# A Mamba block with two MLPs on one core: chunks of 27 and 37 batches, three buffers for B, and one norm's squares ahead of decays

## What is computed

```python
h = _L0_tok_ref(x, L0_tok_W, L0_tok_b)                    # patches @ W.T + b, 512 features
h = h + _L0_attn_ref(_layernorm(h, axis=-1), ...)
h = h + _L0_ffn_ref(_layernorm(h, axis=-1), ...)          # silu(x@gate)*(x@up) @ down, hidden 2048

# inside _L0_attn_ref
zxbcdt = x @ in_proj_w.T
dt = jax.nn.softplus(dt_in @ dt_proj_w.T + dt_proj_b)
dA = jnp.exp(dt[..., None] * A)
def step(h, inp):
    dA_i, dBx_i, C_i = inp
    h = dA_i * h + dBx_i
    y = jnp.einsum('bgn,bgcn->bgc', C_i, h.reshape(b, GC, D_INNER // GC, D_STATE))
y = ys.transpose(1, 0, 2) + D_skip * x_full
h = res + (y * jax.nn.silu(z)) @ out_proj_w.T
return h + mlp(rmsnorm(h))                                # hidden 2048 again
```

## Time and profile before

| | |
|---|---|
| median of 3 runs | 679.44 us (677.98 to 681.44) |
| profiled execution | 676.66 us, of it the span from the first to the last instruction 674.7 us |
| mean granted clock of TensorE | 0.979 of 2.4 GHz |
| busy in the span | PE 630.5, PEld 505.2, DVE 425.5, ACT 329.3, POOL 428.9 us |
| chain that ended last | PE 73%, DVE 12%, ACT 4%, POOL 4%, issue 3%, DMA 2% |
| DMA | 163.50 MB, 242 GB/s over the span |
| loads of B, median from issue to landing | 32 of 580 KB 8.2 us, 32 of 700 KB 6.7 us |
| on the chain at the start | a load of B, 6.61 us from 31.14 |
| on the chain from 212.31 to 235.82 us | GpSimd, its products, additions and softplus one after another |

### The profile page before, as it was taken

The page is one execution under the profiler, slowest core; times in us unless marked ns, Lnnn a source line. Parts: engine busy times, 40 slices in busy tenths (PEclk is TensorE's granted clock), DMA queues, the critical chain, the costliest instruction groups (busy, mean ns, idle before and its releaser), DMA issues.

```text
span 674.7 us, 8618 instructions
## 1 busy us (share of the span) xinstructions
PE 630.5 (93%) x2846; PEld 505.2 (75%) x2846; DVE 425.5 (63%) x660; ACT 329.3 (49%) x646; POOL 428.9 (64%) x244
## 2 busy tenths in 40 slices
PE   4959998799999979999979999999999999999998
PEld 3637675466665657777747777766999998999998
DVE  4087997889987859889887988861322223332132
ACT  4358888458887363323346323321642443543441
POOL 0276786348787999887877988644455464445561
PEclk9979999799999979999989999999999999999999
DMA  8799997599999949989866998634443353144421
GB/s 339 253 358 365 316 312 245 169 280 371 336 375 373 362 176 359 412 334 332 316 247 231 345 326 317 200 124 113 140 153 127 124 157 125 63 128 131 147 67 43
DMA packets 49164, 163.50 MB, mean 242 GB/s; under 512 B 4320, under 2 KB 18528, under 8 KB 48480
## 3 DMA queue, kind: packets, MB, share of 16 engines
q1 hardware_dynamic: 49120, 162.95, 69.6%
HBM read 145.24 MB, written 17.69 MB: 242 GB/s over the span
## 4 chain that ended last, share of the span: by engine, by line
PE 73%; DVE 12%; ACT 4%; POOL 4%; issue 3%; DMA 2%; SPq 0%; DVEq 0%; ACTq 0%; POOLq 0%
PE work L990 53%; PE da L990 15%; DVE da L781 7%; PE work L1000 5%; DVE hs L792 3%; POOL hs L453 2%; ACT L528 1%; DMA bb<-b_rows 1%; ACT da L551 1%; DMA c_rows<-c_rows 1%; DMA sm<-small 1%; POOL acc L479 0%; POOL acc L477 0%; POOL hs L466 0%; DVE a L847 0%
## 5 line engine op out<-in xcount | busy, mean ns | idle before, releaser
L781 DVE TENSOR_TENSOR_SCAN da<-da,hs 128x290 f32<-128x290 f32 (+1 forms) x256 | 198.1, 817 | 35.1 <-POOL hs L453 21.2
L453 POOL TENSOR_TENSOR hs<-dtx,bb 128x1160 f32<-128x1160 f32 (+1 forms) x64 | 171.1, 2674 | 59.6 <-PE work L1000 52.4
L551 ACT ACTIVATE da<-dt,a_neg 128x261 f32<-128x261 f32 (+1 forms) x256 | 118.4, 495 | 144.7 <-DVE hs L792 144.5
L432 POOL TENSOR_TENSOR ws<-wraw,ws 128x1024 fp32r<-128x1024 f32 x40 | 101.5, 2538 | 92.8 <-ACT ws L559 92.8
L990 PE MATMUL work<-sq,wraw 128*128 128x290 f32 x512 | 126.0, 407 | 1.5 <-DVE sq L880 1.1
L990 PE MATMUL work<-hn,win 128*128 128x290 f32 (+1 forms) x336 | 103.6, 457 | 17.4 <-DVE hn L855 8.0
L990 PEld LDWEIGHTS work<-sq,wraw 128*128 128x128 f32 x512 | 96.5, 189 | 30.8 <-issue 1.8
L792 DVE TENSOR_TENSOR hs<-da,cb 128x580 f32<-128x580 f32 (+1 forms) x128 | 105.3, 822 | 10.2 <-DMA cb<-c_rows 3.5
L990 PEld LDWEIGHTS work<-hn,win 128*128 128x128 f32 x336 | 65.7, 200 | 51.3 <-issue 26.1
L559 ACT CAST ws<-wraw 128x1024 fp32r<-128x1024 f32 x48 | 50.3, 1048 | 70.6 <-PE da L990 34.4
L990 PE MATMUL work<-hn,ws 128*128 128x350 f32 x480 | 79.2, 323 | 1.6 <-DVE hn L951 1.6
(11 more groups left out here) (97 smaller groups left out, 630.8 us busy)
## 6 DMA issues: line engine op xcount, KB each, us to landing
wraw<-w_stream SPq DMA_DIRECT2D x104, 512.0 KB, 3.8
bb<-b_rows SPq DMA_DIRECT2D x32, 700.0 KB, 6.7
cb<-c_rows SPq DMA_DIRECT2D x32, 700.0 KB, 5.5
bb<-b_rows SPq DMA_DIRECT2D x32, 580.0 KB, 8.2
cb<-c_rows SPq DMA_DIRECT2D x32, 580.0 KB, 6.2
c_rows<-c_rows SPq DMA_DIRECT2D x8, 875.0 KB, 11.0
c_rows<-c_rows SPq DMA_DIRECT2D x8, 725.0 KB, 6.4
win<-w_in SPq DMA_DIRECT2D x4, 1024.0 KB, 13.1
```

The costliest lines, as they stand in the source:

```text
L432: nc.gpsimd.tensor_tensor(ws[:, k % NW, 1, :], wraw[:, split_loads[k] % NRAW, :], ws[:, k % NW, 0, :].bitcast(F32), ALU.subtract).then_inc ...
L453: nc.gpsimd.tensor_tensor(hs[:, u % NH, 0:NQ * n].rearrange("p (n t) -> p n t", t=n), dtx[:, t % 2, 0:n].unsqueeze(1).to_broadcast([P, NQ, ...
L551: last = nc.scalar.activation(dst, src, ACT.Exp, scale=a_neg[:, j:j + 1])
L781: nc.vector.tensor_tensor_scan(da[:, k % ND, 0:w], da[:, k % ND, 0:w], hs[:, u % NH, p * w:(p + 1) * w], 0.0, ALU.mult, ALU.add).then_inc( ...
```

## The change

The chunks become 27 and 37 batches, 270 and 370 columns; `TM` becomes 370. The ring of B has three buffers, and a slot loads B of unit + 2. On ScalarE a slot whose only `in_z` steps are `SEAM` steps is now cut in the middle like a slot without one, so that the next unit's decays come between its halves. After a silu in a slot with `SEAM` steps the table loaded is the one for exp and tanh.

```diff
-CBS = (29, 35)
+CBS = (27, 37)
...
-NH, NB, ND, NC = 4, 4, 4, 3
+NH, NB, ND, NC = 4, 3, 4, 3
...
                             for u in range(2):
                                 load_b(u)
                                 load_c(u)
-                            load_b(2)
-                if unit is not None and unit + 3 < NCH * UNITS:
-                    load_b(unit + 3)
+                if unit is not None and unit + 2 < NCH * UNITS:
+                    load_b(unit + 2)
                 if unit is not None and unit + 2 < NCH * UNITS:
                     load_c(unit + 2)
...
-                    if not parts and not any(s[0] == "in_z" for s in second):
+                    if not parts and not any(s[0] == "in_z" and s not in SEAM for s in second):
                         n = len(second) // 2
                         first, second = second[:n], second[n:]
...
                 if tables[0] == "silu_and_others" and unit is not None:
-                    log_tables()
+                    use_tables("exp_and_others" if any(s in SEAM for s in steps) else "natural_log_exp_and_others")
```

## The result

The changed kernel takes 683.18 us (680.57 to 685.66, 13 runs); the kernel before, run beside it on the same chip, 678.44 us. The ratio is 1.0069 with a 95% interval of 1.0051 to 1.0087: 3.5 to 5.9 us slower, where 6.0 was forecast. The profiled spans differ by more, 674.7 and 682.4 us, so sums over the two traces come to 7.7 us, 3 more than the medians.

A forecast was written before the change was run, and what follows sets the result against it. TensorE was taken as the bound in the middle part, VectorE and GpSimd close behind; terms for opening, B, crossing, middle and end summed to +6.0 us, 682.7 profiled, median near 685.5 us, range 674.5 to 691.5 (forecast's own 681 to 691.5).

The forecast's parts named there:

- The split matmul: Last part, second chunk's MLPs: 1152 fp32r records each 8.5 ns longer at 370 columns, +9.8 us.
- the filler's 118 ns: 128-column filler matmuls load fresh weights per record at 118 ns, so a weight load cannot be the 161 ns floor.
- 15 ns are not columns as such: Split matmul at 350 columns: one cycle per column gives 146 ns of 161, leaving 15 ns not due to columns.
- Columns in the middle: First chunk's MLPs beside the second recurrence: TensorE sheds 12.8 us, VectorE limits the gain to -6.0 us.
- 77.0 us of work: VectorE from 255 to 340 us: wider operations bring its work to 77.0 us, its floor to 83.0.
- The chunks simply trade: Rival: VectorE's gaps close, TensorE keeps its 12.8 us, or B is not late; 679.5 us, no change; chance 0.18.
- Opening and first recurrence: Until 107 us: about -1.0 for the opening, -3.5 for some 13 narrower units; then +0.3 to 192 us.
- B behind the six tiles: After the weight loads at 191.5 us: B lands late, products start at 210 and 216.4 us, +4.2 us.
- I see two places without it: Loads of B lack slack only at the start, +1.0 us, and behind the six weight loads, +4.2 us.
- B late throughout: Rival: B late in the middle part too, some 25 units losing 0.3 us each, 693 us; chance 0.05.
- The first norm: Squares come 2.6 us earlier, TensorE idle 3 us instead of 5.5; the clock may hold, taken as -1.0.
- The second norm: An exp table load of 1.28 us before the squares, TensorE idle 6.1 us instead of 4.9: +1.3 us.

## Why the prediction was right, point by point

The time, the direction and the range came out, but the nearness of the time is luck: two errors of opposite sign cancel. By part of the change:

| part | forecast, us | measured, us | by |
|---|---|---|---|
| columns | +3.1 | -2.2 (1.6 either way; +0.9 between the traces) | widths against the ring alone |
| ring and place of B | +5.2 | +7.7 (1.2 either way) | the ring alone |
| ScalarE at the norms | -2.3 | -1.5 alone, -0.9 in the change | the edits alone; taken back |
| sum | +6.0 | +4.7 | |

*The split matmul: right.* 1152 records at 8.3 ns more are 9.6 us, against 9.8. The argument from the filler's 118 ns held, and the split records of 128 columns go at 112 ns: a fresh weight load each time does not take the 189 ns that its row shows, since these rows overlap. "15 ns are not columns as such" was wrong: a column costs 0.45 to 0.46 ns, a little more than one cycle of 2.4 GHz, and at most 5 ns are fixed.

*Columns in the middle: right in size, with one wrong step.* The traces of the two kernels that differ in widths alone give -6.8 us, forecast were -6.0. For the change as a whole I forecast -4.7 and the trace has -7.8. The step that failed is "77.0 us of work" for VectorE in the stretch from 255 us, and with it VectorE as the bound: it worked 74.80 us there for 350 records of TensorE and now works 78.04 us for 366, per record the same. The prices had grown as forecast:

```profile
L780 DVE TENSOR_TENSOR_SCAN da<-da,hs 128x370 f32<-128x370 f32 x128 | 113.0, 923 | 19.5 <-POOL hs L452 9.7 <-DVE gated_n L904 3.0 <-DVE h L917 1.5
...
L791 DVE TENSOR_TENSOR hs<-da,cb 128x740 f32<-128x740 f32 x64 | 59.0, 922 | 2.5 <-DVE a L886 0.2
```

But they are durations of records that overlap: in the stretch the durations of all its records add up to 5.9 us more than VectorE's busy time before and to 7.7 us more now, so adding them to a busy time counts too much. That stretch's floor was near 81 us and not 83.0, with the same 6.0 us of gaps. Over the whole middle TensorE is busy 11.3 us less but idle 3.5 us more (7.2 and 10.7 us, 2.1 of it at the second norm), so the outcome lies between the forecast and the rival "The chunks simply trade"; the change was slower all the same, because B was later than forecast. What I had also not seen is how close GpSimd would come to full: 70.94 us and 6 more, in 83, were forecast, 81.73 in 84 came.

*Opening and first recurrence: right per unit, wrong at the start.* The first products with C of the 7th and the 15th unit, before and after:

```profile
67.53 0.76 DVE L792 TENSOR_TENSOR hs<-da,cb 128x580 f32<-128x580 f32 x1
...
105.42 0.76 DVE L792 TENSOR_TENSOR hs<-da,cb 128x580 f32<-128x580 f32 x1
```

```profile
69.70 0.72 DVE L791 TENSOR_TENSOR hs<-da,cb 128x540 f32<-128x540 f32 x1
...
105.64 0.72 DVE L791 TENSOR_TENSOR hs<-da,cb 128x540 f32<-128x540 f32 x1
```

Eight units take 35.94 us and not 37.89, 0.24 us less each where 0.25 was forecast. What was wrong lies ahead of them, where the changed kernel is 2.2 us late and should have been early. After them the gain stops: the 17th unit's product with C starts at 122.9 us, before at 122.8, and in the ring-only kernel at 127.0. With B issued early and the same widths it starts at 117.7 us. At the start 2.4 us are a lower clock in the first 24 records, 8.46 us for 270 columns (granted clock 0.66) where the kernel before took 6.10 for 290 (1.00):

```profile
16.95 6.10 PE L990 MATMUL work<-hn,win 128*128 128x290 f32 x24 [3.55 <-DVE hn L855]
```

```profile
16.98 8.46 PE L989 MATMUL work<-hn,win 128*128 128x270 f32 x24 [3.39 <-DVE hn L854]
```

Why it rose later is open: in the profiled executions four kernels took 5.7 to 6.1 us at this place (the one before among them) and the others 7.4 and more, with no edit that goes with it. The ring-only kernel has it too (7.79 us for its 24 records of 290 columns), but is only 0.1 us behind at its first product with C, so the 2.9 us of its 7th unit come after it.

*B behind the six tiles: right in place and price.* Forecast were 210 and 216.4 us for the two late products; they start at 211.32 and 217.94. The price was +4.2 us, and the ring alone loses 3.9 between its 31st unit and the first norm.

*"I see two places without it": wrong, and the first was priced too low.* At the start +1.0 was forecast with 2 as its bound; the ring alone has lost 2.9 us by its 7th unit. In the changed kernel the fourth product with B waits for the load that stands on the chain from 41.43 us; with B issued early the third and fourth come in one piece:

```profile
48.33 2.28 POOL L452 TENSOR_TENSOR hs<-dtx,bb 128x1080 f32<-128x1080 f32 x1 [3.34 <-DMA bb<-b_rows]
```

```profile
39.52 4.52 POOL L453 TENSOR_TENSOR hs<-dtx,bb 128x1080 f32<-128x1080 f32 x2 [1.02 <-DMA bb<-b_rows]
```

And there is a third place, at 145 to 156 us. I had judged slack by the mean length of a unit, 4.7 and 7.4 us, against the median landing. But units come in bursts: GpSimd takes two at 145.52 at once, and the next B, issued at 144.93, lands 10.8 us later beside a store of B rows and loads of C.

```profile
145.52 4.73 POOL L452 TENSOR_TENSOR hs<-dtx,bb 128x1080 f32<-128x1080 f32 x2 [4.49 <-PE work L999]
155.76 2.30 POOL L452 TENSOR_TENSOR hs<-dtx,bb 128x1080 f32<-128x1080 f32 x1 [5.51 <-DMA bb<-b_rows]
```

Before, the second of these started at 151.72. GpSimd's waits for B grew from 6.0 us to 29.7, in 14 waits:

```profile
POOL hs L452 <- DMA bb<-b_rows: 29.7, 14, 8.0
```

Of these 6.1 us fall before 46 us, where the kernel before waited its 6.0 too, 11.2 between 46 and 195 us (the 3.3 at the start and the 5.5 of the third place among them), 8.7 in two waits behind the tiles, 0.6 from 258 to 342 us and 3.1 after that. Not all of a wait is lost time: between its 17th and its 31st unit, with the third place in it, the ring alone falls back by 1.0 us. The middle has next to none, so "B late throughout" (693) did not come true. The changed kernel's waits for B from 258 to 342 us:

```profile
POOL hs L452 <- DMA bb<-b_rows: 0.6, 1, 0.6
```

*The first norm: right but for the clock.* The idle time fell by 2.6 us on the kernel before, and by 2.6 at the widths of the change, from 7.15 to 4.54. That the change shows only 1.0 less than the 5.52 of before is due to its widths: without the edit the ring alone has 5.04 us there, and with the new widths 7.15. The clock, worth -1.0 in the sum, was not regained. *The second norm: right.* 6.97 us instead of the forecast 6.1, but 1.4 more than the 5.58 without the edits, where 1.3 was forecast; the medians' 2.2 us (1.6 either way) do not contradict it.

## What to carry to other kernels

A load's slack is to be measured by the burst in which its consumer takes buffers and by the slowest landing, not by the mean pace and the median landing. With fewer buffers it can be better to keep the early issue and let the queue wait for the buffer: the place in the queue was worth 5.8 us here (1.6 either way), the buffer itself 2.0 (1.1 either way). A busy time is not to be raised by durations of records that overlap. And before two chunks are shifted against each other, measure the price of a column in both forms of matmul with one kernel of several widths.

## What the runs showed of the hardware

- The fp32r record's spacing is 112 ns at 128 and 200 columns and 0.46 ns per column from 256 to 370; the weight load beside it is recorded with 189 ns and takes no more than 112.
- After 2.78 to 2.96 us of idleness ahead of the first norm TensorE's eight records took 3.83 to 3.88 us, the lower clock level (granted clock 0.54), in three kernels and 2.06 us, the upper level (1.00), in one. So I could not tell by the length of the idle time alone whether the clock is kept.
- A load of B of 700 or 740 KB issued soon after six weight tiles, or after four, stands in the chain with 14.5 to 17.0 us in seven kernels, where the median of the changed kernel's is 7.5 us.
- From 258 to 342 us of the changed kernel GpSimd reached 97% beside a DMA share of 0.99, at 381 GB/s, and TensorE at 100%.
